# Weighted values: the means as two more columns of the q and k product, a reordered chain, and token weights divided at the end

## The reference, cut to what matters

```python
qkv = (x @ qkv_w).reshape(Bx, Nx, 3, Cx)
q, k, v = (qkv[..., 0, :], qkv[..., 1, :], qkv[..., 2, :])
mu_q = q.mean(-1, keepdims=True); mu_k = k.mean(-1, keepdims=True)
dq, dk = (q - mu_q, k - mu_k)
sigma_qk = (dq * dk).sum(-1, keepdims=True) * inv_cm1      # sigma_q2, sigma_k2 alike
num = (2 * mu_q * mu_k + c1) * (2 * sigma_qk + c2)
den = (mu_q ** 2 + mu_k ** 2 + c1) * (sigma_q2 + sigma_k2 + c2)
attn_base = ((num / (den + 1e-07)) ** 2)[..., 0]
A = attn_base + _ode_func(attn_base, ...)   # conv over tokens, group norm, relu, conv
weights = jax.nn.softmax(jax.nn.sigmoid(A), axis=1)         # over the 2048 tokens
ch_w = jax.nn.sigmoid(jax.nn.relu(m @ ch_w1 + ch_b1) @ ch_w2 + ch_b2)   # m: mean over tokens
out_low = weights[..., None] * v * ch_w
return out_low @ proj_w + proj_b
```

## Time and profile before

| | us |
|---|---|
| median of 3 runs | 1781.8 (1781.79 to 1781.89) |
| the profiled execution | 1781.63 |
| its span in the profile | 1779.9 |
| TensorE busy in the span | 1602.2 (90%) |
| VectorE busy | 1274.2 (72%) |
| ScalarE busy | 1208.0 (68%) |
| GpSimd busy | 1180.4 (66%) |

### The profile page before, as it was taken

The page is one execution under the profiler, slowest core; times in us unless marked ns, Lnnn a source line. Parts: engine busy times, 40 slices in busy tenths (PEclk is TensorE's granted clock), DMA queues, the critical chain, the costliest instruction groups (busy, mean ns, idle before and its releaser), DMA issues.

```text
span 1779.9 us, 47951 instructions
## 1 busy us (share of the span) xinstructions
PE 1602.2 (90%) x20135; PEld 1263.7 (71%) x20135; DVE 1274.2 (72%) x1668; ACT 1208.0 (68%) x1880; POOL 1180.4 (66%) x778
## 2 busy tenths in 40 slices
PE   4999978999999999999975966999999999999986
PEld 2777846877777777777752954877777777777764
DVE  4776658887787788787744355887877877777863
ACT  5886864677677777777666455677776776776764
POOL 3010027988878888888833345988888888888861
PEclk8999988999999999999997567999999999999998
DMA  3100001222222222222100001222222222222111
GB/s 87 48 8 1 1 24 45 61 64 50 50 61 52 50 58 50 49 59 50 45 21 0 1 6 35 69 59 50 59 49 56 59 50 52 61 50 52 47 29 54
DMA packets 66146, 78.88 MB, mean 44 GB/s; under 512 B 14146, under 2 KB 41868, under 8 KB 65932
## 3 DMA queue, kind: packets, MB, share of 16 engines
q1 hardware_dynamic: 65932, 75.82, 17.5%
HBM read 23.10 MB, written 2.10 MB: 14 GB/s over the span
## 4 chain that ended last, share of the span: by engine, by line
PE 61%; ACT 17%; DVE 14%; issue 4%; POOL 2%; DMA 1%; DVEq 0%; SPq 0%; POOLq 0%; ACTq 0%
PE PS L195 10%; PE PS L197 9%; PE PS L196 9%; PE PS L718 7%; PE PS L699 4%; DVE t L1036 4%; PE PS L622 3%; PE PS L674 3%; PE PS L681 2%; ACT t L935 2%; DVE t L1042 2%; ACT L965 2%; ACT t L882 2%; ACT L935 2%; DVE t L1099 2%
## 5 line engine op out<-in xcount | busy, mean ns | idle before, releaser
L1195 POOL TENSOR_TENSOR t<-t 128x1024 f32<-128x1024 f32 x128 | 435.5, 3402 | 101.9 <-DVE t L1042 101.8
L1201 POOL TENSOR_TENSOR t<-t 128x512 f32<-128x512 f32 x256 | 321.7, 1278 | 18.6 <-POOL t L1195 0.4
L1092 DVE TENSOR_TENSOR yT<-PS,yT 128x128 f32<-128x128 f32 x128 | 37.3, 292 | 239.7 <-PE PS L718 239.7
L195 PE MATMUL PS<-wqh,HH 128*128 128x512 f32 x384 | 174.7, 455 | 29.6 <-DVE t L1042 17.8
L882 ACT ACTIVATE t<-PS 128x1024 f32<-128x1024 f32 x128 | 131.3, 1026 | 90.5 <-PE PS L681 90.0
L1219 POOL TENSOR_TENSOR HL<-t,HH 114x512 fp32r<-114x512 f32 (+1 forms) x84 | 118.3, 1421 | 104.0 <-ACT HH L949 104.0
L1053 DVE TENSOR_TENSOR t<-t 128x1024 f32<-128x1024 f32 x128 | 176.8, 1381 | 4.4
L850 ACT ACTIVATE t<-PS 128x1024 f32<-128x1024 f32 x128 | 131.3, 1025 | 71.5 <-PE PS L197 71.5
L1063 DVE TENSOR_TENSOR t<-PS,t 128x1024 bf16<-128x1024 f32 x128 | 155.9, 1218 | 20.6 <-ACT t L867 9.1
L1036 DVE TENSOR_REDUCE t<-t 128x16 f32<-128x1024 f32 x128 | 154.8, 1210 | 16.9 <-ACT t L850 16.7
L718 PEld LDWEIGHTS PS<-t,wo 128*128 128x128 f32 x1024 | 132.1, 192 | 35.5 <-issue 14.4
(11 more groups left out here) (255 smaller groups left out, 3917.7 us busy)
## 6 DMA issues: line engine op xcount, KB each, us to landing
t<-t SPq DMA_DIRECT2D x254, 130.0 KB, 2.4
t<-in_c_rope SPq DMA_DIRECT2D x128, 128.0 KB, 2.6
t<-yT SPq DMA_DIRECT2D x112, 128.0 KB, 2.4
t<-in_L_attn_a_x SPq DMA_DIRECT2D x4, 512.0 KB, 6.9
out_x<-t SPq DMA_DIRECT2D x8, 256.0 KB, 3.0
t<-yT SPq DMA_DIRECT2D x16, 127.8 KB, 2.3
t<-in_L_ffn_wqkv SPq DMA_DIRECT2D x2, 768.0 KB, 4.3
t<-in_L_ffn_w SPq DMA_DIRECT2D x2, 341.0 KB, 3.3
```

Of the source, the lines that this page charges most:

```text
L195: e.matmul(o, ah, bh, start=not more, stop=False, skip_group_check=True)
L1195: e.e.tensor_tensor(BL.tc.rearrange("p (x h) d -> p x h d", x=2), BL.qn.rearrange("p (x h) d -> p x h d", x=2), sin.to_broadcast([128, 2, ...
L1201: e.e.tensor_tensor(tv[:, :, 32 * s:32 * s + 32], tv[:, :, 32 * s:32 * s + 32], BL.tc[:, :, 32 * (1 - s):32 * (1 - s) + 32], ALU.add).then ...
```

## The change

Five edits, all in stage 6 and its preparation. The two columns of means are appended to the centred weights (258 columns), so that one product gives both; each tile now has a bank of its own (three pairs of banks in turn), and VectorE copies the 4 means of a step from PSUM (a new semaphore, `wv_mn`, on which TensorE waits too). The copy at the head of the chain goes. The channel sum on VectorE moves ahead of the wait for the neighbours, and its product ahead of the first mean on TensorE. Two loads of ScalarE's function table are written out earlier, and the token sigmoid comes after the third copy. The broadcasts take the exponentials undivided and begin before their sum is known; the sum's average comes between the first and second group of broadcasts, and each multiplication takes in the reciprocal as a scalar, with the factor 1/128 moved to ScalarE's copies.

```diff
-                    BV = Names(wm=arena(sc, [2]), wmh=arena(sc, [2], F32R), wml=arena(sc, [2], F32R),
-                               wce=arena(sc, [2, 128]), wceh=arena(sc, [2, 128], F32R), wcel=arena(sc, [2, 128], F32R))
+                    BV = Names(wce=arena(sc, [258]), wceh=arena(sc, [258], F32R), wcel=arena(sc, [258], F32R))
...
-            e.e.tensor_copy(BV.wmh, BV.wm).then_inc(S.wv_w, 1)
+            e.wait_ge(S.wv_w, 3)
+            e.e.tensor_copy(BV.wceh, BV.wce).then_inc(S.wv_w, 1)
             e.wait_ge(S.wv_w, 4)
-            e.e.tensor_copy(BV.wceh, BV.wce).then_inc(S.wv_w, 1)
-            e.e.tensor_tensor(BV.wml, BV.wm, BV.wmh.bitcast(F32), ALU.subtract).then_inc(S.wv_w, 1)
-            e.wait_ge(S.wv_w, 5)
             e.e.tensor_tensor(BV.wcel, BV.wce, BV.wceh.bitcast(F32), ALU.subtract).then_inc(S.wv_w, 1)
...
             def statistics(j):
-                if j >= 4:
-                    e.wait_ge(S.wv_dd, j - 4 + 1)
+                if j >= 3:
+                    e.wait_ge(S.wv_dd, j - 3 + 1)
+                    e.wait_ge(S.wv_mn, j - 3 + 1)
                 for s in range(2):
                     h, hl = tokens(HH, 2 * j + s), tokens(HL, 2 * j + s)
-                    halves(e.e, PS[:, j % 4, 256 * s:256 * s + 256], h, hl, BV.wceh.rearrange("p a b -> p (a b)"),
-                           BV.wcel.rearrange("p a b -> p (a b)"))
-                    mm = halves(e.e, PS[:, 7, 4 * j + 2 * s:4 * j + 2 * s + 2], h, hl, BV.wmh, BV.wml)
+                    mm = halves(e.e, PS[:, 2 * (j % 3) + s, 0:258], h, hl, BV.wceh, BV.wcel)
                 mm.then_inc(S.wv_p, 1)
...
             e.wait_ge(S.wv_ch, WVC["base"])
             neighbours(BW.w[:, 3, :], 1)
+            e.wait_ge(S.wv_ch, WVC["ych"])
+            e.e.matmul(PS[0:32, 6, 0:2], cw1[:, :], sm[:, 8:10], start=True, stop=True).then_inc(S.wv_cw, 1)
             e.wait_ge(S.wv_ch, WVC["mean0"])
             e.e.matmul(PS[:, 5, 0:8], avg, sm[:, 0:8], start=True, stop=True).then_inc(S.wv_gm, 1)
-            e.wait_ge(S.wv_ch, WVC["ych"])
-            e.e.matmul(PS[0:32, 6, 0:2], cw1[:, :], sm[:, 8:10], start=True, stop=True).then_inc(S.wv_cw, 1)
...
-            e.wait_ge(S.wv_ch, WVC["sums"])
-            e.e.matmul(PS[:, 5, 16:18], avg, sm[:, 22:24], start=True, stop=True, skip_group_check=True).then_inc(S.wv_gm, 1)
-            e.wait_ge(S.wv_ch, WVC["end"])
+            e.wait_ge(S.wv_ex, 1)
             e.wait_ge(S.wv_z, NCH)
             for c in range(NCH):
+                if c == 1:
+                    e.wait_ge(S.wv_ch, WVC["sums"])
+                    e.e.matmul(PS[:, 7, 0:2], avg, sm[:, 22:24], start=True, stop=True).then_inc(S.wv_gm, 1)
+                if c == 7:
+                    e.wait_ge(S.wv_ch, WVC["end"])
                 for j in range(4):
                     t = 4 * c + j
-                    mm = e.e.matmul(PS[:, c, 128 * j:128 * j + 128], BW.w[:, 6, t:t + 1].to_broadcast([128, 128]), ident,
+                    mm = e.e.matmul(PS[:, c, 128 * j:128 * j + 128], BW.w[:, 5, t:t + 1].to_broadcast([128, 128]), ident,
                                     start=True, stop=True, skip_group_check=True)
...
-                e.e.copy(BW.dd[j % 3].rearrange("p a b -> p (a b)"), PS[:, j % 4, :]).then_inc(S.wv_dd, 1)
+                e.e.copy(BW.dd[j % 3].rearrange("p (s a) b -> p s (a b)", s=2),
+                         PS[:, 2 * (j % 3):2 * (j % 3) + 2, 0:256]).then_inc(S.wv_dd, 1)
...
+            e.e.preload_act_table_set("sigmoid_and_others")
             e.wait_ge(S.wv_v, 1)
             e.e.copy(BW.wvT, PS[:, 0, 0:128]).then_inc(S.wv_c, 1)
...
+            e.e.preload_act_table_set("sigmoid_and_others")
             for c in range(NCH):
                 e.wait_ge(S.wv_x, c + 1)
                 e.wait_ge(S.wv_sum, NCH)
-                e.e.copy(BW.P[c], PS[:, c % 3, :]).then_inc(S.wv_z, 1)
-                if c == 3:
+                e.e.activation(BW.P[c], PS[:, c % 3, :], ACT.Copy, scale=1.0 / 128).then_inc(S.wv_z, 1)
+                if c == 2:
                     e.wait_ge(S.wv_ch, WVC["ode"])
...
+                e.wait_ge(S.wv_dd, j + 1)
+                e.e.tensor_copy(st[:, 0:2, 2 * j:2 * j + 2].rearrange("p a b -> p b a"),
+                                PS[:, 2 * q:2 * q + 2, 256:258]).then_inc(S.wv_mn, 1)
                 e.wait_ge(S.wv_sq, j + 1)
...
-            follow(v.tensor_copy(w[:, 7:9, :].rearrange("p a b -> p b a"),
-                                 PS[:, 7, 0:2 * TT].rearrange("p (t a) -> p t a", a=2)))
-            mq, mkk = w[:, 7, :], w[:, 8, :]
+            mq, mkk = st[:, 0, :], st[:, 1, :]
...
             follow(v.tensor_tensor(h4, over(w[:, 3, :]), tap(12, 1), ALU.mult))
+            e.wait_ge(S.wv_sum, NCH)
+            follow(v.tensor_reduce(sm[:, 8:10], BW.ysum.rearrange("p (b c) -> p b c", b=NB), AX.X, ALU.add))
             e.wait_ge(S.wv_nb, 1)
...
-            follow(v.reciprocal(sm[:, 24:26], PS[:, 5, 16:18]))
-            follow(v.scalar_tensor_tensor(w[:, 6, :].rearrange("p (b t) -> p b t", b=NB),
-                                          sm[:, 24:26].rearrange("p (b o) -> p b o", o=1).to_broadcast([128, NB, NT]),
-                                          1.0 / 128, w[:, 5, :].rearrange("p (b t) -> p b t", b=NB), ALU.mult, ALU.mult))
+            follow(v.reciprocal(sm[:, 24:26], PS[:, 7, 0:2]))
...
-                    e.e.tensor_tensor(BW.P[c], PS[:, c, :], BW.P[c], ALU.mult).then_inc(S.wv_pw, 1)
+                    b = c // 4
+                    e.e.scalar_tensor_tensor(BW.P[c], PS[:, c, :], sm[:, 24 + b:25 + b], BW.P[c], ALU.mult,
+                                             ALU.mult).then_inc(S.wv_pw, 1)
```

More of the change, by code:

```diff
@@ L1259, in value_weights_dve @@
             e.wait_ge(S.ld_small, 16 * (len(small) + 2))
-            e.e.tensor_reduce(BV.wm, wb2, AX.X, ALU.add).then_inc(S.wv_w, 1)
+            wm = BV.wce[:, 256:258]
+            e.e.tensor_reduce(wm, wb2, AX.X, ALU.add).then_inc(S.wv_w, 1)
             e.wait_ge(S.wv_w, 1)
-            e.e.tensor_scalar(BV.wm, BV.wm, 1.0 / 128, None, ALU.mult).then_inc(S.wv_w, 1)
+            e.e.tensor_scalar(wm, wm, 1.0 / 128, None, ALU.mult).then_inc(S.wv_w, 1)
             e.wait_ge(S.wv_w, 2)
-            e.e.tensor_tensor(BV.wce, wb2, BV.wm.rearrange("p (a o) -> p a o", o=1).to_broadcast([128, 2, 128]),
+            e.e.tensor_tensor(BV.wce[:, 0:256].rearrange("p (a b) -> p a b", b=128), wb2,
+                              wm.rearrange("p (a o) -> p a o", o=1).to_broadcast([128, 2, 128]),
                               ALU.subtract).then_inc(S.wv_w, 1)
-            e.e.tensor_copy(BV.wmh, BV.wm).then_inc(S.wv_w, 1)
+            e.wait_ge(S.wv_w, 3)
+            e.e.tensor_copy(BV.wceh, BV.wce).then_inc(S.wv_w, 1)
             e.wait_ge(S.wv_w, 4)
-            e.e.tensor_copy(BV.wceh, BV.wce).then_inc(S.wv_w, 1)
-            e.e.tensor_tensor(BV.wml, BV.wm, BV.wmh.bitcast(F32), ALU.subtract).then_inc(S.wv_w, 1)
-            e.wait_ge(S.wv_w, 5)
             e.e.tensor_tensor(BV.wcel, BV.wce, BV.wceh.bitcast(F32), ALU.subtract).then_inc(S.wv_w, 1)
-        WVC = dict(base=14)
-        WVC["mean0"] = WVC["base"] + 5 + 1
-        WVC["ych"] = WVC["mean0"] + 1
-        WVC["mean1"] = WVC["ych"] + 5
+        WVC = dict(base=13)
+        WVC["ych"] = WVC["base"] + 2
+        WVC["mean0"] = WVC["ych"] + 4 + 1
+        WVC["mean1"] = WVC["mean0"] + 5
         WVC["var"] = WVC["mean1"] + 2
@@ L1281, in build @@
         WVC["sums"] = WVC["ode"] + 1
-        WVC["end"] = WVC["sums"] + 2
+        WVC["end"] = WVC["sums"] + 1
         TT = NB * NT
@@ L1318, in weighted_values_pe @@
             e.wait_ge(S.wv_dd, STATS)
+            e.wait_ge(S.wv_mn, STATS)
             e.e.transpose(PS[:, 0, 0:128], wb[:, 256:384], ident).then_inc(S.wv_v, 1)
@@ L1428, in weighted_values_dve @@
                 e.e.tensor_reduce(st[:, 4, 2 * j:2 * j + 2], BW.dm[q], AX.X, ALU.add).then_inc(S.wv_rd, 1)
-            e.wait_ge(S.wv_p, STATS)
             e.wait_ge(S.wv_rd, STATS)
+            e.wait_ge(S.wv_mn, STATS)
             steps = [0]
@@ L1450, in weighted_values_dve @@
             follow(v.tensor_tensor(w[:, 0, :], w[:, 0, :], w[:, 4, :], ALU.mult))
-            follow(v.tensor_tensor(w[:, 1:3, :], w[:, 7:9, :], w[:, 7:9, :], ALU.mult))
+            follow(v.tensor_tensor(w[:, 1:3, :], st[:, 0:2, :], st[:, 0:2, :], ALU.mult))
             follow(v.scalar_tensor_tensor(w[:, 1, :], w[:, 1, :], c1, w[:, 2, :], ALU.add, ALU.add))
@@ L1469, in weighted_values_dve @@
             follow(v.tensor_tensor(h4, over(w[:, 3, :]), tap(12, 1), ALU.mult))
+            e.wait_ge(S.wv_sum, NCH)
+            follow(v.tensor_reduce(sm[:, 8:10], BW.ysum.rearrange("p (b c) -> p b c", b=NB), AX.X, ALU.add))
+            assert steps[0] == WVC["ych"]
             e.wait_ge(S.wv_nb, 1)
@@ L1477, in weighted_values_dve @@
             assert steps[0] == WVC["mean0"]
-            e.wait_ge(S.wv_sum, NCH)
```

(2 more changed lines are left out.)

2 lines of the change are left out of this document (1 added, 1 removed).

## The result

The changed kernel takes 1754.3 us (median of 4 runs, 1753.5 to 1755.3), the kernel before 1781.8 beside it (4 runs, 1781.1 to 1781.9): the ratio is 0.9847, with a 95% interval of 0.983 to 0.9864. The forecast was 1755.1. The profiled execution after took 1753.49 us with a span of 1751.7, so 28.2 us less span than before (1779.9).

The account below looks back on a forecast made before the run. TensorE at 1.2 GHz was taken to bound the stage's first half, the chain's length the rest; savings 21.8 + 0 + 0.1 + 1.3 + 1.3 + 2.2 = 26.7 off 1781.8 gave 1755.1 us, range 1752.0 to 1761.0.

Parts of the forecast that it names:

- 1. Means in the same product: Statistics: 96 two-column products go, the others grow to 258 columns, and the clock rises after four steps; -21.8 us.
- TensorE waiting for VectorE's copy of the means: Statistics: listed among the signs that would show the prediction wrong; no size given.
- 2. The copy at the head: Head of the chain after the statistics: the removed copy gains 0, as the next multiplication meets GpSimd's same addition; bound 0.85 us.
- 3. Preparation: Layer-norm stage ahead: VectorE's 2-column weight operations go and a wait comes; -0.1 us, between 0 and -0.3.
- 4. First sigmoid: Channel gate: moving the table load into ScalarE's idle time brings its work up to the Exp earlier; -1.3 us.
- 5. Second sigmoid and the start of the broadcasts: Before the broadcasts: earlier table load, sigmoid after three copies, broadcasts not waiting for sums; -1.3 us, bounds -0.5 and -1.7.
- 6. Broadcast and division: First broadcast to last addition: shorter TensorE pause keeps the clock high, 9.8 us for 12.03; -2.2, or +0.75 at low clock.
- Low broadcasts: Rival: the broadcasts of token weights stay at 1.2 GHz, giving 1758.4 us; chance 0.18.
- No rise in the statistics: Rival: the clock never rises in the statistics and stays low in the rest, giving 1760.2 us; chance 0.10.
- No cheap form: Rival: in the statistics, 258 columns take two slots of 256, step stays 2.56 us, giving 1776.9 us; chance 0.03.
- The ring: Rival: in the statistics, the means' copy holds PSUM banks until each step runs as one chain, 1797 us; chance 0.03.

Follow-up runs that it names:

- number 6: Changed kernel without VectorE's copy of the means and TensorE's wait for it, constants standing in for the means; 1753.2 us (one run).
- number 3: Kernel before with its 96 two-column products made 256 columns wide, the extra results unread; 1764.58 us, ratio 0.9895 to the kernel before.
- number 1: Changed kernel with the separate 2-column products, their weights' preparation and the copy at the head of the chain put back; 1776.38 us, ratio 0.9966 to the kernel before.
- Number 2: Kernel before with only the merged 258-column product and its copies, without the copy at the head; 1760.56 us, ratio 0.9876 to the kernel before.
- Number 9: Changed kernel with the addition of the projection's bias moved from GpSimd to ScalarE; 1753.97 us, ratio 0.9841 to the kernel before.
- Number 4: Changed kernel without both early sigmoid table loads, token sigmoid back behind the fourth copy, new gate order kept; 1759.32 us, ratio 0.9873 to the kernel before.
- number 10: Changed kernel with early table loads kept, but the channel sum and the product with cw1 back behind the first average; 1752.97 us (one run).
- number 5: Changed kernel with average, reciprocal and scaling back ahead of all broadcasts, plain copies and multiplications; 1754.00 us, ratio 0.9839 to the kernel before.
- 8: Changed kernel with ScalarE squaring only a quarter of the columns and without the copy of the means; 1751.4 us (one run).
- 11: Changed kernel with bias on ScalarE, scaling ahead of the broadcasts, and token sigmoid as tanh after the first copy; 1752.23 us, ratio 0.9841 to the kernel before.
- 7: Changed kernel with ScalarE squaring only a quarter of the columns of each step, other squares left out; 1752.4 us (one run).

## Why the prediction was right, and where its steps were not

**1. Means in the same product** (-21.8; measured -22.2). Right in size and in mechanism: the clock rises at 983.1, the step then goes from TensorE to ScalarE (1.14 for a forecast 1.17), the copy of the means takes 0.155 (0.2) and is hidden, and the ring of three pairs holds nobody up for long. One of the prediction's signs of being wrong did show, TensorE waiting for VectorE's copy of the means (1.8 us in all); it cost nothing, since without that wait and that copy the statistics take 20.19 (number 6). The rise was argued from back-to-back wide products elsewhere; number 3 shows it directly. How much of the term is the clock and how much the smaller number of products depends on which is taken first (number 3). On the doubt there, that the Trainium skill, "TensorE: Matmul & The Clock Gate", Part 1, lets sustained activity alone raise the clock: the trace disagrees in the kernel before, with 40.8 of 41.0 us busy at 0.50, and in number 1, with 40.4 of 40.4, and agrees where all products are wide.

**2. The copy at the head** (0, bound -0.85; measured -0.25). Number 2, with the product and without the copy, takes 13.30 for a stretch that takes 13.55 before; number 1 and the kernel after differ by the same 0.25. The step that failed was that the multiplication, 0.3 earlier, meets the same addition of GpSimd and ends with it. It began instead at 1000.99, just ahead of GpSimd's second addition at 1001.01, and took 0.19; the operation behind it was held until that addition ended (0.90 for 0.24). Number 9 shows it by taking GpSimd away. The rule of the Trainium skill, "SBUF — State Buffer", "Who interferes with whom", that the first to issue wins, agrees with the 0.19 of the multiplication; I had applied it to the wrong instruction. The operation that took 0.90 has one tensor and a scalar from SBUF, so the prediction's wording, two SBUF inputs, doesn't clearly take it in; that GpSimd held it rests on number 9.

**3. Preparation** (-0.1): -0.06 in the layer norm ahead of the stage. The rest of the 0.43 ahead was there before that layer norm began, and is not the change's.

**4. First sigmoid** (-1.3; measured -1.25). The size is right and the mechanism is not. (The 1.25 is 13.30 of number 2, which has the product and not the copy at the head, less 12.05.) The step that failed is "Without the load everything that ScalarE does from there up to the Exp comes 1.28 earlier". Number 4 puts the load back and loses nothing: it lies in ScalarE's wait for the product with cw2. What brings the Ln forward is the order, as the product with cw1 no longer stands behind the average and its inputs (number 10). The prediction named this edit and gave it no price; that the one it did price gave nearly the same figure is chance.

**5. Second sigmoid and the start of the broadcasts** (-1.3; measured -1.53). In number 4, without the early load, Ln to first broadcast is 13.94, as in the kernel before (13.89); in number 5, without the new order of sums and broadcasts, it is 12.32, as after. So the whole term is the load and the place of the sigmoid, and the freedom from average, reciprocal and scaling, which the prediction counted in, gives nothing: the last copy ends later than they would. The load and the place of the sigmoid were only taken back together, so their shares are open.

**6. Broadcast and division** (-2.2; measured -2.00). That the clock stays up was the forecast, and the reason given, the shorter pause ahead, fits, though no run changed the pause alone: number 4 has a pause of 2.30 us again, then 0.52 in the broadcasts and 12.46, which is 0.43 more than before (the prediction had +0.75 for this case). But the gain is the clock's alone. At the high clock the old form takes 9.52 and the new one 10.03 (number 5), so division at the end costs 0.5.

**The rivals.** Low broadcasts: false for the kernel after, and true for number 4. No rise in the statistics: false, and true for number 1. No cheap form: false, since 258 columns take about the slot of 256 (0.215 us from start to start between 980.12 and 983.13 in the kernel after, against 0.2135). The ring: false, as said under 1, with 1.8 us of waiting in 20.2.

**Open.** The stages behind gave 0.5 us more, which no run explains and which is within what whole runs differ by. Why products x reach the quicker pace 4.8 to 5.6 us after the scaling by the group norm in the kernels before and after and in numbers 3, 4, 5, 6, 8 and 11, but 6.2 to 7.8 us after it in numbers 1, 2, 7, 9 and 10, isn't shown either. The chains of the second group are the longer ones where one edit is compared (0.42 to 0.86 over the kernel after in 1, 7, 9 and 10), so differences in the chain of less than 1 us are not put down to an edit's own work.

## What to carry to other kernels

Count products, not columns, where many are narrow, and look at the granted clock beside the busy time: an engine that is "full" at half its clock is worth two questions: can there be fewer of its products, and what keeps its clock down. Here an edit that only let the clock rise took 16 us off a stage in which the whole change took off 27. When a load of a table is moved, find what its engine would wait for at the old place; if that ends later, the load was free there. And price each reordering on its own, since several edits that go together can hide that one of them (here the division at the end, +0.5) costs.

## What the runs showed that I had not expected

- More arithmetic made the kernel faster: 96 products widened from 2 to 256 columns took 16.4 us off the stage (number 3), 16.3 of them in the statistics, where the clock rose, with TensorE counted busy in both cases.
- An operation of VectorE with a scalar from SBUF was held by GpSimd's addition like one with two tensors (0.90 against 0.24), while the copy of the means out of PSUM took 0.155 beside GpSimd's products.
- Where the clock rises inside a chain moves by 1 to 3 us between kernels that differ little, and it took back part of what was gained ahead of it in number 9 (0.42 in the chain of the 0.68 in head and gate).
